# Local attention in 32x32 tiles: blocks of 32 keys by 64 queries, chunk by chunk

## What is computed

```python
def local_gqa_attn(x, wq, wk, wv, wo):      # H = 16 heads of HD = 8, KVH = 4, WIN = 32
    q = split_heads(x @ wq, H)
    k = split_heads(x @ wk, KVH)
    v = split_heads(x @ wv, KVH)
    q, k = (rope(q, BASE_L), rope(k, BASE_L))
    q, k = (qk_norm(q), qk_norm(k))
    k, v = (repeat_kv(k), repeat_kv(v))
    i = jnp.arange(x.shape[1])
    diff = i[:, None] - i[None, :]
    mask = (diff >= 0) & (diff < WIN)
    return merge_heads(sdpa(q, k, v, mask)) @ wo
```

## Time and profile before

| | |
|---|---|
| median of 3 runs | 1047.9 us (1047.13 to 1048.45) |
| the profiled execution | 1043.13 us, of which the span is 1041.0 us |
| mean granted TensorE clock | 0.945 |
| busy share of the span | PE 91%, PEld 42%, DVE 51%, ACT 52%, POOL 14% |
| chain that ended last, by engine | PE 78%, ACT 8%, DVE 6% |
| GpSimd, numerators of 1024 columns (L707) | 2.85 us |
| local stage: VectorE's mask (L1324), group keys (L1276), additions (L1317) | 1.76, 0.75, 0.66 us each |
| a set of the local stage | 3.64 us |

### The profile page before, as it was taken

How to read it: one execution, slowest core, us unless ns; L and a number is a source line. 1 busy time by engine, 2 the same in 40 slices (tenths; PEclk the granted TensorE clock), 3 DMA queues, 4 the chain that set the end, 5 groups by cost and what they waited for, 6 DMA issues and landing times.

```text
span 1041.0 us, 23939 instructions
## 1 busy us (share of the span) xinstructions
PE 949.4 (91%) x10552; PEld 442.3 (42%) x10552; DVE 535.3 (51%) x870; ACT 541.9 (52%) x767; POOL 146.2 (14%) x164
## 2 busy tenths in 40 slices
PE   7489969899999988997899799997999999999998
PEld 4257743423333335883333334433333333344443
DVE  4356725733333266665465445546666666423554
ACT  6024445689999946443655551246454454445121
POOL 4101020331001003110011040000233223004000
PEclk9789999999999998559999899999999999998999
DMA  7653140010000000000000036400000000001651
GB/s 205 202 150 101 53 169 0 0 42 2 2 2 2 2 1 2 4 4 1 1 0 0 1 76 150 104 1 0 2 3 2 2 2 2 0 1 29 160 130 51
DMA packets 16479, 43.23 MB, mean 42 GB/s; under 512 B 4812, under 2 KB 5260, under 8 KB 14700
## 3 DMA queue, kind: packets, MB, share of 16 engines
q1 hardware_dynamic: 16376, 41.71, 14.7%
HBM read 36.91 MB, written 4.55 MB: 40 GB/s over the span
## 4 chain that ended last, share of the span: by engine, by line
PE 78%; ACT 8%; DVE 6%; issue 2%; DMA 2%; SPq 2%; POOL 1%; DVEq 0%; POOLq 0%
PE ps L1599 77%; ACT nrr L816 2%; ACT nrr L814 1%; DMA stf<-aux 1%; ACT work L1059 1%; POOL work L665 1%; SPq L578 1%; ACT work L860 0%; DVE mxq L1220 0%; DVE work L1553 0%; ACT nrr L803 0%; ACT nrr L800 0%; DVE stf L1567 0%; SPq L572 0%; DMA stf<-scr_k 0%
## 5 line engine op out<-in xcount | busy, mean ns | idle before, releaser
L1599 PE MATMUL ps<-rq,stf 32*64 32x512 f32 (+4 forms) x4096 | 213.5, 469 | 3.5 <-ACT hz L964 1.6
L1599 PE MATMUL ps<-work,vbuf 64*32 64x96 f32 (+6 forms) x3712 | 197.2, 386 | 2.4 <-issue 2.2
L1599 PE MATMUL ps<-hz,wsb 128*128 128x512 f32 (+1 forms) x352 | 159.3, 608 | 6.3 <-ACT nsq L805 3.5
L1599 PEld LDWEIGHTS ps<-rq,stf 32*64 32x64 f32 x4096 | 102.1, 152 | 108.4 <-issue 85.8
L920 ACT ACTIVATE work<-ps 128x1024 f32<-128x1024 f32 x144 | 139.4, 1022 | 13.4 <-PE ps L1599 10.0
L1599 PEld LDWEIGHTS ps<-work,vbuf 64*32 64x32 f32 (+1 forms) x3712 | 72.5, 121 | 112.6 <-issue 65.2
L982 ACT ACTIVATE work<-ps 128x1024 f32<-128x1024 f32 x72 | 73.6, 1024 | 75.7 <-PE ps L1599 75.7
L1599 PEld LDWEIGHTS ps<-hz,wsb 128*128 128x128 f32 (+1 forms) x352 | 61.7, 188 | 86.2 <-issue 67.5
L1301 DVE TENSOR_TENSOR work<-work,csb 128x1024 f32<-128x1024 f32 (+1 forms) x40 | 41.6, 1040 | 95.8 <-ACT work L920 95.4
L1028 ACT ACTIVATE work<-ps 128x512 f32<-128x512 f32 x48 | 28.7, 597 | 117.2 <-PE ps L1599 117.2
L1599 PE MATMUL ps<-work,wsb 128*128 128x512 f32 (+1 forms) x176 | 86.9, 602 | 2.7 <-DVE work L1514 2.7
(11 more groups left out here) (194 smaller groups left out, 1163.4 us busy)
## 6 DMA issues: line engine op xcount, KB each, us to landing
stf<-scr_w SPq DMA_DIRECT2D x32, 256.0 KB, 4.5
stf<-scr_w SPq DMA_DIRECT2D x64, 128.0 KB, 3.4
stf<-scr_k SPq DMA_DIRECT2D x12, 204.0 KB
stf<-scr_q SPq DMA_DIRECT2D x12, 192.0 KB
wsb<-in_w SPq DMA_DIRECT2D x1, 2192.0 KB, 11.0
rq<-in_rq SPq DMA_DIRECT2D x2, 1024.0 KB, 8.2
scr_q<-work SPq DMA_DIRECT2D x6, 256.0 KB, 5.1
scr_k<-work SPq DMA_DIRECT2D x6, 256.0 KB, 5.6
```

Of the source, the lines that this page charges most:

```text
L1599: return nc.tensor.matmul(o, l, r, start=start, stop=stop, skip_group_check=True)
```

## The change

A block has QB = 32 keys and W_L = 64 queries. Scores and values both use 32x32 tiles of the array, four blocks to a key tile, one for each 32 partitions: 2 pairs x 4 x 4 x 2 = 64 score matmuls and 4 x 4 x 4 = 64 value matmuls in a set, of 64 columns each. Sets go chunk by chunk, with the four groups inside (`LOCAL_SETS`), so there are 16 sets as before; keys of a group are made one chunk (512 columns) at a time, three sets ahead. The results of a chunk stand in banks 4 to 7, one bank for each block position, both group pairs side by side. Each chunk ends with two copies on ScalarE and four operations on VectorE, one of which carries the last 32 columns over to the next chunk (`spill`). The numerators are picked in three parts. `nsq` and `nrr` become two halves of one buffer.

```diff
+QB = P // 4
-W_A, W_L = P + WIN_A, HB + WIN_L
+W_A, W_L = P + WIN_A, QB + WIN_L
...
+        rows2 = sb("rows2", [P, 2, NC, CH], F32)
+        nsq, nrr = rows2[:, 0], rows2[:, 1]
+        spill = sb("spill", [P, 2, W_L - QB], F32)
...
+        LOCAL_SETS = [(c, g) for c in range(NC) for g in range(NG)]
+        def local_cells(c):
+            return both_out[:, :, c * CH:(c + 1) * CH].rearrange("p k (t s) -> p k t s", s=P)
+        def local_block(blk):
+            return bank(4 + blk).rearrange("p (k t s) -> p k t s", k=2, t=4)
...
-            for b in range(B):
-                even_pair_numerators(AL, b)
+            for lo, hi in ((0, 2), (2, 3), (3, 4)):
+                pool.wait_ge(q["oc"], WAS[AL]["oc"] + hi)
+                nc.gpsimd.tensor_scalar(nums[:, lo * CH:hi * CH], half_out[0][:, lo * CH:hi * CH],
+                                        c_("part")[:, 0:1], None, ALU.mult).then_inc(q["sel"], 1)
...
+                def copy_even(c):
+                    act.wait_ge(q["pv"], was["pv"] + NG * (c + 1))
+                    for blk in (0, 2):
+                        ins = nc.scalar.activation(local_cells(c)[:, :, :, QB * blk:QB * blk + W_L], local_block(blk),
+                                                   ACT.Copy)
+                    ins.then_inc(q["oe"], 1)
...
-                    if n % 4 == 1 and n > 1:
-                        copy_even(n // 2 - 1)
+                    if n % NG == 1 and n > 1:
+                        copy_even(n // NG - 1)
...
+                def add_odd(c):
+                    dve.wait_ge(q["oe"], was["oe"] + c + 1)
+                    first = local_cells(c)[:, :, :, QB:QB + W_L]
+                    nc.vector.tensor_tensor(first, local_block(1), first, ALU.add)
+                    lo, hi = c * CH + 3 * QB, (c + 1) * CH
+                    third = both_out[:, :, lo:hi - QB].rearrange("p k (t s) -> p k t s", s=P)[:, :, :, 0:W_L]
+                    nc.vector.tensor_tensor(third, local_block(3)[:, :, 0:3], third, ALU.add)
+                    if c % CB:
+                        dve.wait_ge(q["oc"], was["oc"] + c)
+                        begin = both_out[:, :, c * CH:c * CH + W_L - QB]
+                        nc.vector.tensor_tensor(begin, spill[:], begin, ALU.add)
+                    else:
+                        nc.vector.tensor_copy(spill[:], local_block(3)[:, :, 3, QB:W_L])
+                    last = both_out[:, :, hi - QB:hi]
+                    nc.vector.tensor_tensor(last, local_block(3)[:, :, 3, 0:QB], last, ALU.add).then_inc(q["oc"], 1)
+                def chunk_keys(n):
+                    c, g = LOCAL_SETS[n]
+                    if g == 1 or n == NG * CB:
+                        dve.wait_ge(q["kn"], was["kn"] + c + 1)
+                    nc.vector.tensor_scalar(kz[:, g, c * CH:(c + 1) * CH], ch(kn, c), group_mask(g), None,
+                                            ALU.mult).then_inc(q["kz"], 1)
+                chunk_keys(1)
+                chunk_keys(2)
...
-                dve.wait_ge(q["sel"], was["sel"] + 2)
-                dve.wait_ge(q["oc"], was["oc"] + (COPIES[a] if a == AL else COPIES[a] - NC + c + 1))
+                dve.wait_ge(q["sel"], was["sel"] + (c if a == AL else 2))
+                dve.wait_ge(q["oc"], was["oc"] + COPIES[a] - NC + c + 1)
...
                 def scores(n):
-                    b, g = PASSES[n // 2]
-                    if n % 2 == 0 and g == 0:
-                        pe.wait_ge(q["q"], was["q"] + min(NC, CB * (b + 1) + 1))
-                    if n % 2 == 0:
-                        pe.wait_ge(q["kz"], was["kz"] + keys_of(AL, n // 2))
+                    c, g = LOCAL_SETS[n]
+                    if g == 0:
+                        pe.wait_ge(q["q"], was["q"] + min(NC, c + 2))
+                    pe.wait_ge(q["kz"], was["kz"] + local_keys(n))
...
-                            for half in range(2):
-                                at = k0 + HB * half
+                            for blk in range(4):
+                                at = c * CH + j * P + QB * blk
                                 for hd in (2 * pair, 2 * pair + 1):
                                     rows = slice(32 * hd, 32 * hd + 32)
-                                    ins = mm(bank(hd)[HB * half:HB * (half + 1), j * W_L:(j + 1) * W_L],
-                                             kz[rows, g, at:at + HB], qd[rows, at:at + W_L])
+                                    ins = mm(bank(hd)[QB * blk:QB * (blk + 1), j * W_L:(j + 1) * W_L],
+                                             kz[rows, g, at:at + QB], qd[rows, at:at + W_L])
...
                 def values(n):
-                    if n % 4 == 0 and n:
-                        pe.wait_ge(q["oc"], was["oc"] + n // 4)
+                    if g == 0 and n:
+                        pe.wait_ge(q["oc"], was["oc"] + c)
                     for j in range(4):
+                        for blk in range(4):
+                            rows = slice(QB * blk, QB * (blk + 1))
+                            at = c % CB * CH + j * P + QB * blk
+                            w = min(W_L, S - at)
+                            for hd in range(G):
+                                ins = mm(local_block(blk)[32 * hd:32 * hd + 32, g // 2, j, 0:w],
+                                         vq[rows, 4 * c + j, g // 2, g % 2],
+                                         probs_of(n)[rows, hd, j * W_L:j * W_L + w], g == 0 and j == 0, False)
...
-    ahead = np.arange(W_L)[None, :] - i[:, None] % HB
+    ahead = np.arange(W_L)[None, :] - i[:, None] % QB
```

More of the change, by code:

```diff
@@ L125, in build @@
         qd = rq[:, 2 * S:2 * S + T + WIN_L]
-        nsq = sb("nsq", [P, NC, CH], F32)
-        nrr = sb("nrr", [P, NC, CH], F32)
+        rows2 = sb("rows2", [P, 2, NC, CH], F32)
+        nsq, nrr = rows2[:, 0], rows2[:, 1]
+        spill = sb("spill", [P, 2, W_L - QB], F32)
         vbuf = sb("vbuf", [P, B * KT * H * VW], F32)
@@ L150, in build @@
         probs = work[:].rearrange("p (n h s) -> p n h s", n=4, h=G)
-        half_out = [t[:].rearrange("p c s -> p (c s)") for t in (nsq, nrr)]
+        both_out = rows2[:].rearrange("p k c s -> p k (c s)")
+        half_out = [both_out[:, k] for k in range(2)]
         guess, inverse = aux[:, 0:CH], aux[:, CH:2 * CH]
@@ L324, in build @@
                              each=8, o=5)
-        LOCAL_COUNTS = dict(GLOBAL_COUNTS, sc=32, ex=32, mk=16, pv=16, oe=4, oc=4, o=6)
+        LOCAL_COUNTS = dict(GLOBAL_COUNTS, kz=16, sc=32, ex=32, mk=16, pv=16, oe=4, oc=4, sel=3, o=6)
         WAS = {a: {k: sum(n.get(k, 0) for n in (WINDOW_COUNTS, GLOBAL_COUNTS, LOCAL_COUNTS)[0:a]) for k in q}
@@ L931, in local_soft @@
                 was = WAS[AL]
[L933 to L942, removed]
+                def copy_even(c):
[4 more added lines that the diff above has]
+                    ins.then_inc(q["oe"], 1)
+                for n in range(len(LOCAL_SETS)):
                     rotated_consumed(AL, n)
@@ L950, in local_soft @@
                                              ps[:, 2 * k:2 * k + 2, 0:w], ACT.Exp, scale=SCALE).then_inc(q["ex"], 1)
-                    if n % 4 == 1 and n > 1:
-                        copy_even(n // 2 - 1)
+                    if n % NG == 1 and n > 1:
+                        copy_even(n // NG - 1)
                 reciprocal_guess(AL, 0)
-                copy_even(len(PASSES) - 1)
+                copy_even(NC - 1)
                 reciprocal_guess(AL, 1)
@@ L1324, in local_attention @@
                     nc.vector.tensor_tensor(cells, cells, band, ALU.mult).then_inc(q["mk"], 1)
[L1325 to L1328, removed]
+                    if n % NG == 1 and n > 1:
+                        add_odd(n // NG - 1)
+                    if n + 3 < len(LOCAL_SETS) and n + 3 != NG:
+                        chunk_keys(n + 3)
                     if n == 12:
                         first_numerators(AL)
-                add_odd(len(PASSES) - 1)
+                add_odd(NC - 1)
             def relu_heads():
@@ L1798, in keys_of, with local_keys @@
                 return CB + k
+            def local_keys(n):
+                return 1 if n == 0 else 2 if n == NG else n + 2 if n < NG else n + 1
             def causal_attention(a):
@@ L1879, in scores @@
                         for j in range(4):
-                            k0 = b * S + (4 * (n % 2) + j) * P
-                            for half in range(2):
-                                at = k0 + HB * half
+                            for blk in range(4):
+                                at = c * CH + j * P + QB * blk
                                 for hd in (2 * pair, 2 * pair + 1):
                                     rows = slice(32 * hd, 32 * hd + 32)
-                                    ins = mm(bank(hd)[HB * half:HB * (half + 1), j * W_L:(j + 1) * W_L],
-                                             kz[rows, g, at:at + HB], qd[rows, at:at + W_L])
```

(18 more changed lines are left out.)

## The result

The changed kernel takes 1102.17 us (median of 4 runs, 1098.67 to 1105.53), the kernel before 1047.52 beside it (1043.37 to 1048.45). The ratio is 1.051, 95% interval 1.0467 to 1.0553: **slower by 5.1%**. The forecast was 1094 us, 1062 to 1112. The profiled execution took 1098.67 us, its span is 1096.7 us, 55.7 more than before.

What follows compares the result with a forecast made beforehand. Late instruction blocks for TensorE in the local stage were taken as the bound: 1043.1 us profiled + 45.1 for blocks + 0.9 at the last chunk's end = 1089.1; with the median 4.8 above, 1094 us, range 1062 to 1112.

Steps and rivals of the forecast that it cites:

- The bound: Local stage: late instruction blocks set TensorE's pace, 108.9 us against 63.8, +45.1 us; chance 0.80, including only four tiles busy.
- Latency: Local stage: an instruction block is usable 2.4 to 2.9 us after it begins; 2.5 us taken.
- Time from a block's arrival to the next request: Local stage: 125 instructions, or 31 matmuls at 26.7 ns, run before the next request; 0.85 us in a 3.35 us cycle.
- The count at 431.6 us: Kernel before's local stage: some 130 TensorE instructions left after a block begins, from 53 score and about 13 value records with loads.
- Number of blocks: Local stage: 8192 instructions at 255 a block give 32.1 blocks, 32.5 with waits.
- The array's price: Local stage with instructions there: scores 26.7 ns a matmul, values 13.3 to 26.7; a set 2.6 to 3.4 us.
- Tail: Last chunk's end, without cover: additions of 1.6 us for 0.66 on the path to the denominators, +0.9 us.
- Start: Set 2 no longer waits for a whole batch row's keys, where TensorE loses 0.9 us; no gain under late blocks.
- ScalarE, VectorE, GpSimd: Local stage: exponentials 0.60 us, mask 1.23, group keys 0.47, beside TensorE; GpSimd's numerators nothing, 0 to 0.5 us in range.
- Blocks that keep up: Rival, local stage: blocks asked for earlier, array sets pace, sets 2.6 to 3.4 us, 1038 to 1047 us; chance 0.12.
- Requests that follow one another: Rival, local stage: next block asked for once one has come, 2.4 us cycle, 78 us, 1063 us total; chance 0.08.
- Only four tiles busy: Rival, local stage: 53 ns a matmul, 6.8 us a set, 110 us in all; its chance is within late blocks' 0.80.

Runs made afterwards that it cites:

- the first three experiments: Changed kernel with 96 columns a matmul: 1102.53 us; changed kernel with half the instructions, 128 columns: 1047.8 us; kernel before with 64 columns: 1051.04 us.
- the fourth experiment: Changed kernel's chunk-by-chunk order with the kernel before's 64x96 blocks and instruction count: 1048.4 us, ratio 0.9987 against the kernel before.

## Why the prediction was right, point by point

*The bound.* Right: the queue of instructions, not the array, and in the expected form (32 blocks, a comb of two teeth a set, 1.2 GHz, ScalarE and VectorE waiting for TensorE). The experiments carry it: half the instructions took the whole loss away, a quarter fewer took half of it, 50% more columns added little or nothing, a third fewer brought nothing.

*Latency.* 2.5 us was taken, 2.5 measured on average, within 2.2 to 2.9.

*Time from a block's arrival to the next request.* **This term was mis-sized**: 0.85 us was taken, 3.63 - 2.5 = 1.13 was measured. A matmul in a burst costs 27.4 ns (above), close to the 26.7 priced. What was off is the supply in hand: 1.13 us at 27.4 ns are 41 matmuls, some 165 instructions before the next block begins where the forecast had 125, so about 90 are left of a block, not 130. The count at 431.6 us was right for the kernel before: 69 records start there between the block's begin and the stop. What failed is that it was carried over as a constant. Counted in the same way over their holes, the kernel with 128 columns has 64 records on average, that with 96 columns 49, and the kernel after 42. So the faster the records go, the fewer are left when the next block begins. That would follow if the request went out some time before the block begins, but no run shows the request itself. Cycle 3.63 for 3.35, stage 114.7 for 108.9: +50.9 in place of +45.1.

*Number of blocks.* 32.5 forecast, 32 measured.

*The array's price.* Sixteen tiles in values gave 14 ns a record, as eight do in scores, so the lower end (13.3 ns a matmul) is not reached in these bursts, and the upper one (26.7) nearly is. At 27.4 to 28 ns a set of 128 matmuls would take 3.5 to 3.6 us, against 3.64 in the kernel before: by this estimate the change would have brought next to nothing even with instructions at hand. The Trainium skill (TensorE: Matmul & The Clock Gate, Part 3) has sixteen such tiles in one matmul's length plus 4 ns a tile, and by that, as an estimate, a round of values would be 0.17 us; the value records of the burst above (14 ns each, 16 in a round, 0.22 us) do not show it. But columns alone don't set the pace within a burst: with 128 of them a burst of 128 records takes 2.87 us, which less a record's own 0.41 is 19.4 ns each, not twice the 13.7 with 64. The loads or the supply of instructions may set it there, and no run here parts them.

*Tail.* The additions measured 0.69 + 0.55 + 0.22 + 0.22 = 1.68 us (1.6 forecast), on the path as expected; but they overlap there, and take 1.43 us of it (525.61 to 527.04), so the path grew by 0.8 us where 0.9 was forecast. The clock was kept at 1.2 GHz in the sum's stage, and its part behind the stage stood only in the range. It came true. The denominators' 24 matmuls, of the kernel before, where the clock was back at 2.4 GHz:

```profile
473.56 1.75 PE ps L1599 x24
```

They take 3.14 us now (527.09, above). Before, the granted clock was 1.00 from 470 us on; after, it stayed at 1.2 GHz through the 11.1 us behind the stage (0.50, second row of the busy times), though TensorE had stood still for 40% of the stage.

*Start.* "Under late blocks it gains nothing": it lost 1.7 us, the scores starting at 409.65 in place of 407.94. The profiles vary there by more: the same point lies at 406.7, 409.9 and 415.7 us in the first three experiments, whose programs differ from the kernel that they start from only behind that point. It is no effect of the change that these runs can show.

*ScalarE, VectorE, GpSimd.* As priced: exponentials 600 ns, mask 1225 and keys 480 ns, in the cover of TensorE. Without the cover (half the instructions) a chunk's end does come onto the chain, which the forecast put at 1.4 us each (TensorE stands for 1.4 us before 430.84 there, at the first of them).

*The rivals.* Blocks that keep up: no, holes behind each burst. Requests that follow one another: no, 3.63 us between blocks in place of 2.4. Only four tiles busy: no, 13.5 ns a record inside a burst. The sum against the profiled execution was 1043.1 + 46.0 = 1089.1; it took 1098.67. Of the 9.6 us, 5.8 are the block cycle, 1.7 the start and 1.4 the denominators' clock; 0.7 stays open.

## What to carry to other kernels

Count TensorE's instructions as well as its columns: an f32 matmul is four, a block holds some 250, and a long stream of small matmuls got on average no more than one block in 3.4 to 3.8 us in all of these kernels, 13 to 15 ns an instruction and 53 to 60 ns an f32 matmul, with 64, 96 or 128 columns and at either clock. Cutting a block-diagonal problem finer saves columns and doubles instructions; look in the queue "instruction" first, and compare its blocks' spacing in the stage with that figure. Where the stage already stands there, what pays is fewer instructions: wider tiles, or a type whose matmul is one record with one load.

## What the runs showed of the hardware

- A block of 16 KB is usable 2.2 to 2.9 us after it begins, while its packet takes 1.15 us of that (2.0% of 16 engines' 114.7 us, for 32 packets); the rest, 1.3 us or so, lies outside the packet.
- Longer matmuls hardly change the pace, since the holes take up what the bursts gain: 3.63 us a tooth with 64 columns, 3.8 with 96 and 3.8 with half as many instructions of 128 columns.
- A doubled clock is worth little to such a stream (some 9% in the stretch from 436.3 us of the fourth experiment), and a TensorE idle for 40% of a stage still ended it at 1.2 GHz.
- How many instructions are left when a block begins is no constant: 69 records at 431.6 us in the kernel before, 42 on average in the kernel after.
